# ScalarE's share of two chunk steps one tile behind VectorE's, squares and Hadamard steps by single tiles, and a Newton iteration moved from GpSimd to ScalarE

## Chip, cores and metric

One core of one Trainium2 chip runs the whole kernel. The metric is the device time of one execution in microseconds, lower is better. TensorE is called PE, VectorE DVE, ScalarE ACT and GpSimd POOL, as in the profile; SP is the engine that issues most DMAs.

## What is computed

The input x is (4, 512, 512) in float32. It is layer-normed to xn, and the output is `x + xn + mamba2(xn) + ffn(xn)`:

```python
z, xBC, dt = split(xn @ w_in)                  # 1024, 1280, 16 columns
xBC = silu(causal_conv4(xBC) + conv_b)         # x heads 1024, B 128, C 128
dt = softplus(dt + dt_bias)
y = ssd(xh * dt, dt * A, B, C) + xh * D        # a scan, in chunks
y = y * silu(z)
y = y * rsqrt(mean(y * y) + 1e-5) * norm_w
mamba = y @ w_out
ffn = (fwht(silu(xn @ W1.T) * (xn @ W3.T))) @ W2.T     # 2048 hidden columns
```

The Walsh-Hadamard transform (`fwht`) is folded into W2 once.

## The kernel before

**Precision.** Products run on PE in three float16 matmuls per float32 product (`three`, line 600): high by high, high by low, low by high. Each weight tile is scaled by a power of two, which comes from sums of squares of a group of tiles: steps `SQ` square raw tiles on ACT (line 1008), `QS` reduces them on PE and makes the scale on DVE (`to_scale`, signal `scale_13`). Then ACT writes the high half of a tile (`split_hi`, line 924) and DVE the low half (`split_lo`, line 1194), four tiles ahead of PE. This is done in batch 0 only; batches 1 to 3 load the split tiles back (66 of them).

**Tiles.** Per batch there are 10 `C` tiles (convolved columns; numbers 8 and 9 are B and C), 8 `Z` tiles (the gate), 16 pairs `A`, `U` (FFN gate and up) and 16 steps `G` (FFN down). A tile of the first four kinds is 12 matmuls of 128x512, about 2.6 us of PE. A `C` tile is evicted by ACT (line 968), by three taps on DVE (line 1244), then tanh on ACT (line 983) and a product on DVE (line 1229); a `Z` or `A` tile by tanh on ACT (line 973) and a product on DVE (lines 1255, 1260); a `U` tile by a product on DVE (line 1265), its high half on ACT (line 978) and the low half on POOL (line 1443). From the middle of a batch on three PSUM banks rotate for them.

**Steps.** Between the tiles stand steps, each with one part per engine:
- `DT`, `DTL`, `SUM`: dt, in the order PE, DVE (line 1146), ACT (lines 865, 867), POOL; then `DTL` with Ln on ACT, behind a load of its function table (line 871), and DVE's lines 1153 to 1161, whose last gives `dt_a`; `SUM` is PE's cumulative sums of it (lines 634 to 638, waiting on `dt_a`) and ACT's exponentials, for which `F0` waits (`ecst_ok`).
- `F0` to `F7` and `H0` to `H15`: the Hadamard transform of W2 in two passes. `H` is one matmul on bank 4 (line 751), evicted by ACT (line 1028) and DVE (line 1324). `H` number i waits on PE until `H` number i-1 is evicted.
- For each chunk c of 128 rows: `T` transposes, `X` exponentials, `S` and `R` states, `E`, `ES` decay rows, `Y` output (DVE gates it, lines 1365 and 1368; ACT squares it, line 1083), `N`, `Q`, `V` norms (ACT scales y, line 1087), `ROW` three Newton steps of 1/sqrt on one column (POOL), `W` the product with w_out (24 matmuls on the shared bank 3).
- `WOQ`, `WOS`, `WOH`: squares, scale and halves of w_out (line 1333 is the low half, 8 of them). `LN`, `XT` prepare the next batch: `LN` is DVE's statistics (lines 1120 to 1131) and ACT's normalisation (line 853, four operations).

**The order** is one list for all engines, `SCHEDULES[b]`. For batch 0 its head is written out in `FIRST`; after that a step stands at a tile number, out of `FIRST_AT`, `STEP_FIRST`, `ES_FIRST` and `PREP_FIRST`, and steps of one tile number are sorted by a rank (`LN` and `H` have the same rank and then sort by name, so an `H` of tile number 35 stands ahead of `LN`, one of 36 behind it). Every engine walks the list in this order, each instruction in its queue, and waits on semaphores where it needs another's work. Batches 1 to 3 use `STEP_AT` in the same way.

Of the kernel before, what the change touches and what calls it, by code (L numbers as in the profile page):

```python
# [216 lines left out]
def build(nc, x, w_in, w_dt, w1, w3, w2, w_out, conv_w, conv_b, dt_bias, a_log, d_cols, norm_w, consts, out):  # L217
# [6 lines left out]
    with ctx:  # L224
# [664 lines left out]
        def _(act):  # L889
# [49 lines left out]
            for b in range(NB):  # L939
# [45 lines left out]
                for kind, i in SCHEDULES[b]:  # L985
# [11 lines left out]
                    elif kind == "SQ":  # L997
                        act.wait_ge(d_quad[i], 32)
                        if i == 0:
                            act.wait_ge(sq_g1, G1_ACT)  # L1000
# [2 lines left out]
                        junk = sq_act[i >= QUADS_EARLY]
                        for half_of in range(2):
                            if i not in (0, QUADS_EARLY):
                                act.wait_ge(sq_quads, 2 * i + half_of - 1)
                            column = SQ_Q + 2 * i + half_of
                            nc.scalar.activation(junk[:, half_of * 2 * TILE:(half_of + 1) * 2 * TILE].rearrange("p (s c) -> p s c", s=2),
                                                 raw_load_view(i, half_of), ACT.Square,
                                                 accum_out=row_sq[:, column:column + 1]).then_inc(sq_quads, 1)  # L1010
# [540 lines left out]
```

## Time and profile before

| | |
|---|---|
| median of 3 runs | 967.67 us (966.13 to 968.0) |
| the profiled execution's own time | 965.39 us |
| its span, first to last instruction | 963.6 us |
| PE, DVE, ACT, POOL busy | 934.7, 555.8, 391.4, 276.1 us |
| mean granted clock of TensorE | 0.996 of full |

Busy time is the sum of what an engine's instructions cover. An idle stretch in front of an instruction is put down to the one that released it. The durations of matmuls overlap, so starts are the better measure on PE.

### The profile page before, as it was taken

What the parts mean: (1) busy time and instruction counts of PE and PEld (TensorE: products, weight loads), DVE (VectorE), ACT (ScalarE), POOL (GpSimd) and SP (SyncE); (2) the same over time, 40 slices, a digit from 0 to 9 for tenths busy, and PEclk for the clock granted to TensorE, in tenths of its full rate; (3) what the DMA queues carried; (4) which work ended last, traced back from release to release, by engine and by line L of the source; (5) the groups of instructions that cost most, each with busy time, mean ns of one, the idle gap of its engine ahead of it and who ended that gap; (6) DMA issues with size and microseconds to landing.
All of it is one profiled execution on the core that took longest, in us unless ns stands there. A gap on an engine that the chain in (4) does not pass through costs nothing.

```text
span 963.6 us, 13435 instructions
## 1 busy us (share of the span) xinstructions
PE 934.7 (97%) x5000; PEld 469.3 (49%) x5000; DVE 555.8 (58%) x955; ACT 391.4 (41%) x690; POOL 276.1 (29%) x354
## 2 busy tenths in 40 slices
PE   9899987989899999999999999999999999999998
PEld 4444443545344445555454445555445445555543
DVE  7876588875534756556532766566451666575421
ACT  6678874533323445233221434233222444343200
POOL 0000446352000116466110106565210104654410
PEclk9999999999999999999999999999999999999999
DMA  9798355434224335525223435436223435256123
GB/s 336 247 349 295 112 192 193 131 124 137 96 74 147 125 111 159 155 72 176 88 67 113 143 99 164 145 97 175 78 76 101 143 107 160 65 151 153 45 77 98
DMA packets 76208, 134.26 MB, mean 139 GB/s; under 512 B 7536, under 2 KB 20464, under 8 KB 74096
## 3 DMA queue, kind: packets, MB, share of 16 engines
q1 hardware_dynamic: 56640, 104.88, 34.1%
q10 hardware_dynamic: 19504, 28.53, 10.0%
q8 instruction: 40, 0.66, 0.3%
q14 instruction: 24, 0.20, 0.1%
HBM read 107.43 MB, written 25.95 MB: 138 GB/s over the span
## 4 chain that ended last, share of the span: by engine, by line
PE 67%; DVE 1%; DMA 1%; ACT 1%; issue 0%; DVEq 0%; ACTq 0%
PE ps L600 46%; PE ps L834 14%; PE ps L796 2%; PE ps L782 1%; PE ps L788 1%; PE ps L768 1%; DMA arena<-cs_rows 1%; PE ps L619 0%; PE ps L638 0%; PE ps L751 0%; PE ps L771 0%; DVE arena L1348 0%; DVE arena L1426 0%; ACT arena L1059 0%; DVE arena L1265 0%
## 5 line engine op out<-in xcount | busy, mean ns | idle before, releaser
L600 PE MATMUL ps<-xh,arena 128*128 128x512 f16 x1592 | 487.9, 379 | 3.4 <-DVE arena L1194 3.3
L600 PE MATMUL ps<-xl,arena 128*128 128x512 f16 x796 | 302.0, 379 | 0.0
L600 PEld LDWEIGHTS ps<-xh,arena 128*128 128x128 f16 x1592 | 158.3, 99 | 190.3 <-issue 5.9
L834 PE MATMUL ps<-arena 128*128 128x512 f16 x768 | 171.1, 379 | 0.0
L1443 POOL TENSOR_TENSOR arena<-arena 128x512 f16<-128x512 f32 x64 | 71.2, 1113 | 334.6 <-ACT arena L978 334.6
L1244 DVE SCALAR_TENSOR_TENSOR arena<-ps,cw,arena 128x511 f32<-128x511 f32 (+2 forms) x120 | 89.4, 747 | 66.9 <-ACT arena L968 65.0
L600 PEld LDWEIGHTS ps<-xl,arena 128*128 128x128 f16 x796 | 77.9, 98 | 88.7 <-issue 3.3
L834 PEld LDWEIGHTS ps<-arena 128*128 128x128 f16 x768 | 74.1, 98 | 91.2 <-issue 5.5
L978 ACT ACTIVATE arena<-arena 128x512 f16<-128x512 f32 x64 | 40.2, 629 | 141.3 <-DVE arena L1265 141.3
L1260 DVE SCALAR_TENSOR_TENSOR arena<-arena,ps 128x512 f32<-128x512 f32 x64 | 44.0, 687 | 77.3 <-ACT arena L973 77.0
L600 PE MATMUL ps<-wo_hi,arena 128*128 128x512 f16 x256 | 79.9, 384 | 3.6 <-DVE wo_lo L1333 3.4
L973 ACT ACTIVATE arena<-ps,f 128x512 f32<-128x512 f32 x64 | 43.4, 678 | 85.0 <-PE ps L600 85.0
L1454 POOL TENSOR_TENSOR arena<-arena 128x1024 f32<-128x1024 f32 x16 | 30.7, 1920 | 112.5 <-DMA arena<-cs_rows 112.5
L1265 DVE SCALAR_TENSOR_TENSOR arena<-ps,arena 128x512 f32<-128x512 f32 x64 | 44.1, 689 | 24.6 <-PE ps L600 23.3
L1348 DVE TENSOR_TENSOR arena<-arena 128x2048 f32<-128x2048 f32 x16 | 40.5, 2528 | 19.9 <-ACT arena L1074 19.9
L600 PE MATMUL ps<-wo_lo,arena 128*128 128x512 f16 x128 | 49.3, 385 | 0.0
L600 PEld LDWEIGHTS ps<-wo_hi,arena 128*128 128x128 f16 x256 | 25.3, 99 | 37.1 <-DVE wo_lo L1333 3.9
L1059 ACT ACTIVATE arena<-arena 128x128 f32<-128x128 f32 x128 | 40.5, 389 | 5.8 <-DMA arena<-cs_rows 5.8
L1194 DVE SCALAR_TENSOR_TENSOR arena<-arena,scl 128x512 f16<-128x512 f32 x50 | 38.7, 778 | 5.8 <-ACT arena L924 5.8
L924 ACT ACTIVATE arena<-arena,scl 128x512 f16<-128x512 f32 x50 | 35.3, 711 | 12.8 <-DVE f L1308 5.9
L968 ACT ACTIVATE arena<-ps,cb,cw 128x512 f32<-128x512 f32 x40 | 30.8, 771 | 23.1 <-PE ps L600 22.1
L1426 DVE SCALAR_TENSOR_TENSOR arena<-ps,f_w,arena 128x512 f32<-128x512 f32 x16 | 10.9, 745 | 50.3 <-PE ps L834 50.3
(179 smaller groups left out, 1092.8 us busy)
## 6 DMA issues: line engine op xcount, KB each, us to landing
arena<-w_parts SPq DMA_DIRECT2D x198, 256.0 KB, 2.6
w_parts<-arena SPq DMA_DIRECT2D x66, 256.0 KB, 2.6
arena<-cs_rows ACTq DMA_DIRECT2D x16, 1024.0 KB, 5.7
arena<-w SPq DMA_DIRECT2D x24, 512.0 KB, 4.9
arena<-ecs_rows ACTq DMA_DIRECT2D x24, 256.0 KB, 6.9
arena<-x ACTq DMA_DIRECT2D x18, 256.0 KB, 3.4
w_mid<-arena SPq DMA_DIRECT2D x8, 512.0 KB, 3.5
arena<-w_mid SPq DMA_DIRECT2D x16, 256.0 KB, 2.6
```

The lines of the kernel that those rows point to most:

```text
L600: ins = nc.tensor.matmul(out_ap, lhs(i, a), rhs(i, c), start=(i == 0 and s == 0), stop=(i == n - 1 and s == 2))
L834: ins = nc.tensor.matmul(bank(t), hw[a][:, i, t * P:(t + 1) * P], w2s[i % W2R][:, d, :], start=(i == 0 and s == 0), stop=(i == JF - 1 and ...
L924: nc.scalar.activation(part_hi[p % PARTS], raw_tile(p), ACT.Copy, scale=scl[:, n:n + 1]).then_inc(w_hi.sem, 1)
L973: nc.scalar.activation(slot, src, ACT.Tanh, scale=f_half[:, 0:1] if kind == "Z" else f_13[:, i // 2:i // 2 + 1]).then_inc(tanh_ok.sem, 1)
L978: nc.scalar.activation(hid_hi[:, i, :], hs[i % 2], ACT.Copy).then_inc(hid_h.sem, 1)
L1059: ins = nc.scalar.activation(Eb[:, h, :], csbc[:, h, :], ACT.Relu, scale=-1.0, bias=cs_s[:, c * NH + h:c * NH + h + 1])
L1194: nc.vector.scalar_tensor_tensor(out=part_lo[p % PARTS], in0=raw_tile(p), scalar=scl[:, n:n + 1], in1=part_hi[p % PARTS], op0=ALU.mult, op ...
L1244: ins = nc.vector.scalar_tensor_tensor(out=a[:, s:L], in0=src[:, 0:L - s], scalar=cw[:, i, TAPS - 1 - s:TAPS - s], in1=a[:, s:L], op0=ALU. ...
L1260: nc.vector.scalar_tensor_tensor(out=hs[i % 2], in0=tb[tanh[key] % 2], scalar=1.0, in1=src, op0=ALU.add, op1=ALU.mult).then_inc(evac.sem, 1)
L1265: nc.vector.scalar_tensor_tensor(out=hs[i % 2], in0=src, scalar=HID / (2 * XS * XS), in1=hs[i % 2], op0=ALU.mult, op1=ALU.mult).then_inc(e ...
L1348: nc.vector.tensor_tensor(Eb, Eb, Gm.unsqueeze(1).to_broadcast([P, NH, P]), ALU.mult).then_inc(m_ok.sem, 1)
L1443: nc.gpsimd.tensor_tensor(hid_lo[:, i, :], hs[i % 2], hid_hi[:, i, :], ALU.subtract).then_inc(hid_l.sem, 1)
```

## The change

In the head of batch 0, `DT` goes from in front of `C2` to behind it, `DTL` from behind `C2` to behind `Z1`, and `SUM` from behind `C4` to in front of it. A step `SQ` is now one half (two tiles) of what it was, so there are 16, and the second half stands one or two tiles behind the first. The Hadamard steps `H` stand at tile numbers 31 to 46, one each (before 30 to 46, two at 35 and none at 36 and 37). ACT's parts of `Y` and `N` are steps of their own, `YS` and `NS`, which in batch 0 stand behind `Y` and `N` by a tile; in batches 1 to 3 they stand at the same place. `QS6` moves ahead of `R1` (tile 18), `W0` goes from 18 to 19, `N1` and `Q1` from 20 to 21, and PE's waits follow: `W0` waits for `scale_13` at 7 and not 6. `ROW` moves from POOL (12 operations) to ACT (9), in all batches.

```diff
-FIRST = ("B G1S C C0 G1N C1 Z0 DT C2 DTL Z1 C3 Z2 C4 SUM Z3 WOL F0 C5 F1 SQ0 Z4 F2 C6 F3 QS0 Z5 F4 C7 F5 SQ1 Z6 F6 Z7 F7 QS1 E0 A0").split()
+FIRST = ("B G1S C C0 G1N C1 Z0 C2 DT Z1 DTL C3 Z2 SUM C4 Z3 WOL F0 C5 F1 SQ0 Z4 SQ1 F2 C6 F3 QS0 Z5 F4 C7 F5 SQ2 Z6 SQ3 F6 Z7 F7 QS1 E0 A0").split()
...
-            [("SQ", 2, 1), ("QS", 2, 3), ("SQ", 3, 4), ("QS", 3, 7), ("SQ", 4, 8), ("QS", 4, 12), ("SQ", 5, 11), ("QS", 5, 14),
-             ("SQ", 6, 16), ("QS", 6, 20), ("SQ", 7, 20), ("QS", 7, 23)] +
+            [("SQ", n, at) for n, at in enumerate((1, 2, 4, 5, 7, 8, 11, 12, 15, 16, 19, 20), 4)] +
+            [("QS", q, at) for q, at in enumerate((3, 7, 12, 14, 18, 23), 2)] +
...
-            [("H", j, at) for j, at in enumerate((30, 31, 32, 33, 34, 35, 35, 38, 39, 40, 41, 42, 43, 44, 45, 46))])
+            [("H", j, at) for j, at in enumerate(range(31, 31 + JF))])
...
-              "Y": (9, 17, 26, 34), "N": (12, 20, 28, 37), "Q": (12, 20, 28, 37), "V": (14, 23, 30, 39), "W": (18, 25, 31, 41),
-              "ROW": (15, 24, 31, 40)}
+              "Y": (9, 17, 26, 34), "YS": (10, 18, 27, 35), "N": (12, 21, 28, 37),
+              "NS": (13, 22, 29, 38), "Q": (12, 21, 28, 37), "V": (14, 23, 30, 39), "W": (19, 25, 31, 41), "ROW": (15, 24, 31, 40)}
...
                         elif i == 6:
-                            pe.wait_ge(mamba_evac.sem, mamba_evac.at(0, 0))
+                            pe.wait_ge(mean_read.sem, mean_read.at(0, 0))
...
-                            pe.wait_ge(scale_13, 6)
+                            pe.wait_ge(scale_13, 7)
...
+                    elif kind == "ROW":
+                        act.wait_ge(guess_ok.sem, guess_ok.at(b, c))
+                        for n in range(3):
+                            k = steps.step(nc.scalar.activation(ntmp, nr, ACT.Square))
+                            act.wait_ge(steps.sem, k)
+                            k = steps.step(nc.scalar.activation(ntmp, ntmp, ACT.Identity, scale=nmh, bias=three_halves[:, 0:1]))
+                            act.wait_ge(steps.sem, k)
+                            ins = nc.scalar.activation(nr, ntmp, ACT.Copy, scale=nr)
+                            if n < 2:
+                                k = steps.step(ins)
+                                act.wait_ge(steps.sem, k)
+                        ins.then_inc(root_ok.sem, 1)
...
-                    elif kind == "Y":
+                    elif kind == "YS":
...
-                    elif kind == "N":
+                    elif kind == "NS":
```

The order on DVE at the head of batch 0, from the silu product of `C0` on, before the change (line 1244 is the taps of `C2`, line 1146 `DT`, lines 1153 to 1161 `DTL`, line 1255 the eviction of `Z1`, line 1194 the splits):

```order
L1229 SCALAR_TENSOR_TENSOR arena<-arena 128x512
L1146 SCALAR_TENSOR_TENSOR arena<-ps,f_in,dtb 128x64
L1244 SCALAR_TENSOR_TENSOR arena<-ps,cw,arena 128x511
L1229 SCALAR_TENSOR_TENSOR arena<-arena 128x512
L1244 SCALAR_TENSOR_TENSOR arena<-ps,cw,arena 128x510
L1244 SCALAR_TENSOR_TENSOR arena<-ps,cw,arena 128x509
L1194 SCALAR_TENSOR_TENSOR arena<-arena,scl 128x512
L1153 RECIPROCAL arena<-arena 128x64
L1155 TENSOR_TENSOR arena<-arena 128x64
```

And in the changed kernel, whose line numbers are 12 or 13 higher here (1242 for 1229, 1257 for 1244, 1158 for 1146, 1268 for 1255, 1165 for 1153):

```order
L1242 SCALAR_TENSOR_TENSOR arena<-arena 128x512
L1257 SCALAR_TENSOR_TENSOR arena<-ps,cw,arena 128x511
L1242 SCALAR_TENSOR_TENSOR arena<-arena 128x512
L1257 SCALAR_TENSOR_TENSOR arena<-ps,cw,arena 128x510
L1257 SCALAR_TENSOR_TENSOR arena<-ps,cw,arena 128x509
L1207 SCALAR_TENSOR_TENSOR arena<-arena,scl 128x512
L1158 SCALAR_TENSOR_TENSOR arena<-ps,f_in,dtb 128x64
L1268 SCALAR_TENSOR_TENSOR arena<-arena,ps 128x512
L1207 SCALAR_TENSOR_TENSOR arena<-arena,scl 128x512
L1165 RECIPROCAL arena<-arena 128x64
L1167 TENSOR_TENSOR arena<-arena 128x64
```

`DT` stands behind all of `C2` and its split, and `DTL` behind `Z1` and another split.

The order on ACT at the end of batch 0, before: exponentials `X3` (lines 1072, 1074), `H3` and `H4`, the square of `Y3` (1083), `H5` and `H6`, the normalisation of `LN1` (853), `N3`'s scaling of y (1087), and the other `H`:

```order
L1072 ACTIVATE arena<-arena 128x1024
L1074 ACTIVATE arena<-arena 128x1024
L1028 ACTIVATE arena<-ps,f_had 128x512 x2
L1083 ACTIVATE arena<-arena 128x1024
L1028 ACTIVATE arena<-ps,f_had 128x512 x2
L853 ACTIVATE arena<-arena 128x512 x4
L1087 ACTIVATE arena<-arena 128x1024
L1028 ACTIVATE arena<-ps,f_had 128x512 x5
```

And in the changed kernel (1084 and 1086 for 1072 and 1074, 1095 for 1083, 855 for 853, 1099 for 1087):

```order
L1084 ACTIVATE arena<-arena 128x1024
L1086 ACTIVATE arena<-arena 128x1024
L1028 ACTIVATE arena<-ps,f_had 128x512 x3
L855 ACTIVATE arena<-arena 128x512 x4
L1095 ACTIVATE arena<-arena 128x1024
L1028 ACTIVATE arena<-ps,f_had 128x512 x3
L1099 ACTIVATE arena<-arena 128x1024
L1028 ACTIVATE arena<-ps,f_had 128x512 x2
```

The three ahead of the normalisation are now `H2` to `H4`; `H5` and the square of `Y3` stand behind it.

## Rows read from the trace of the kernel before

**Rows 1.** The page, busy us, share of the span, instructions of each engine

```profile
PE 934.7 (97%) x5000; PEld 469.3 (49%) x5000; DVE 555.8 (58%) x955; ACT 391.4 (41%) x690; POOL 276.1 (29%) x354
```

**Rows 2.** Stretches of 24 us: length, busy PE, PEld, DVE, ACT, POOL, clock, DMA, GB/s

```profile
24.00:48.00 24.00, 20.57 (x138) 9.75 (x138) 19.96 (x39) 16.47 (x26) 1.11 (x3) 1.00 0.72 247
...
120.00:144.00 24.00, 20.09 (x103) 11.79 (x104) 19.61 (x41) 16.93 (x35) 10.59 (x7) 0.93 0.60 191
144.00:168.00 24.00, 18.43 (x98) 8.48 (x97) 19.97 (x24) 12.53 (x21) 14.11 (x18) 0.93 0.59 193
...
312.00:336.00 24.00, 24.00 (x113) 10.92 (x112) 17.47 (x25) 12.16 (x23) 3.26 (x2) 1.00 0.42 138
```

**Rows 3.** Timeline of PE, front: start, duration, line, and the idle time before

```profile
42.33 0.38 PE L600 MATMUL ps<-xh,arena 128*128 128x512 f16 x1
45.08 0.39 PE L600 MATMUL ps<-xh,arena 128*128 128x512 f16 x1 [2.37 <-DVE arena L1194]
...
53.73 1.96 PE L719 MATMUL ps<-arena,hads 128*128 128x512 f32 x4 [1.60 <-issue]
```

**Rows 4.** Timeline of ACT, front, from the tanh step of C1 to Ln

```profile
39.20 0.63 ACT L983 ACTIVATE arena<-arena 128x512 f32<-128x512 f32 x1 [3.27 <-DVE arena L1229]
39.73 0.24 ACT L865 ACTIVATE arena<-arena 128x64 f32<-128x64 f32 x1
40.00 0.26 ACT L867 ACTIVATE arena<-arena 128x64 f32<-128x64 f32 x1
40.17 0.71 ACT L924 ACTIVATE arena<-arena,scl 128x512 f16<-128x512 f32 x1
40.78 0.76 ACT L968 ACTIVATE arena<-ps,cb,cw 128x512 f32<-128x512 f32 x1
41.56 1.28 ACT L871 ACT_TABLE_LOAD   x1
42.85 0.26 ACT L871 ACTIVATE arena<-arena 128x64 f32<-128x64 f32 x1
```

**Rows 5.** Timeline of DVE, front: the taps of C2, then DTL

```profile
41.57 0.75 DVE L1244 SCALAR_TENSOR_TENSOR arena<-ps,cw,arena 128x511 f32<-128x511 f32 x1 [2.22 <-ACT arena L968]
...
44.94 0.54 DVE L1153 RECIPROCAL arena<-arena 128x64 f32<-128x64 f32 x1
...
45.66 0.22 DVE L1157 SCALAR_TENSOR_TENSOR arena<-arena 128x64 f32<-128x64 f32 x1
...
46.17 0.23 DVE L1161 TENSOR_TENSOR arena<-arena,nega 128x64 f32<-128x64 f32 x1
```

**Rows 6.** Timeline of PE, middle: the first product with w_out, the tile after

```profile
160.53 0.50 PE L600 MATMUL ps<-wo_hi,arena 128*128 128x512 f16 x1 [3.43 <-DVE wo_lo L1333]
...
167.41 0.38 PE L600 MATMUL ps<-xh,arena 128*128 128x512 f16 x1
```

**Rows 7.** ACT's squares in the groups by line (busy, mean ns); DVE's timeline, middle

```profile
L1008 ACT ACTIVATE arena<-arena 128x1024 bf16<-128x1024 f32 x16 | 16.7, 1045 | 0.0
...
127.05 0.75 DVE L1194 SCALAR_TENSOR_TENSOR arena<-arena,scl 128x512 f16<-128x512 f32 x1 [1.29 <-ACT arena L924]
...
159.73 0.74 DVE L1333 SCALAR_TENSOR_TENSOR wo_lo<-arena,nws,wo_hi 128x512 f16<-128x512 f32 x1
...
162.84 0.68 DVE L1265 SCALAR_TENSOR_TENSOR arena<-ps,arena 128x512 f32<-128x512 f32 x1
```

**Rows 8.** Timeline of PE, tail: the H matmuls that wait

```profile
216.00 1.10 PE L751 MATMUL ps<-arena,hads 128*128 128x512 f32 x2 [2.31 <-issue]
...
245.27 1.13 PE L751 MATMUL ps<-arena,hads 128*128 128x512 f32 x2 [1.62 <-DVE arena L1324]
...
258.85 1.12 PE L751 MATMUL ps<-arena,hads 128*128 128x512 f32 x2 [1.07 <-DVE arena L1324]
```

**Rows 9.** Timelines of DVE and ACT, tail: LN1's first step, the normalisation

```profile
247.82 2.46 DVE L1120 BATCH_NORM_STATS2 arena<-arena 128x6 f32<-128x512 f32 x4
...
253.47 2.94 ACT L853 ACTIVATE arena<-arena 128x512 f32<-128x512 f32 x4 [6.35 <-DVE arena L1131]
```

More of the change, by code:

```diff
@@ L62 @@
     "Y": (6, 14, 22, 32),
+    "YS": (6, 14, 22, 32),
     "N": (8, 16, 24, 34),
+    "NS": (8, 16, 24, 34),
     "Q": (8, 16, 24, 34),
@@ L233, in build @@
         ident, tri_le, tri_gt, ones = (con[:, i * P:(i + 1) * P] for i in range(4))
-        cmean = sb("cmean", [P, 1])
+        cmean, three_halves = sb("cmean", [P, 1]), sb("three_halves", [P, 1])
         hads = sb("hads", [P, 2 * P])
@@ L997, in _ @@
                     elif kind == "SQ":
-                        act.wait_ge(d_quad[i], 32)
+                        quad, half_of = divmod(i, 2)
+                        act.wait_ge(d_quad[quad], 32)
                         if i == 0:
                             act.wait_ge(sq_g1, G1_ACT)
-                        elif i == QUADS_EARLY:
+                        elif i == 2 * QUADS_EARLY:
                             act.wait_ge(xt_done.sem, xt_done.at(0, MC - 1))
[L1003 to L1010, printed above, removed]
+                        if quad not in (0, QUADS_EARLY):
+                            act.wait_ge(sq_quads, i - 1)
+                        junk = sq_act[quad >= QUADS_EARLY][:, half_of * 2 * TILE:(half_of + 1) * 2 * TILE]
+                        nc.scalar.activation(junk.rearrange("p (s c) -> p s c", s=2), raw_load_view(quad, half_of), ACT.Square,
+                                             accum_out=row_sq[:, SQ_Q + i:SQ_Q + i + 1]).then_inc(sq_quads, 1)
                     elif kind == "F":
@@ L1166, in _ @@
             steps = Steps(dve_steps)
+            nc.vector.memset(three_halves[:], 1.5)
             nc.vector.memset(row_sq[:], 2.0 ** -60).then_inc(guards, 1)
@@ L1299, in _ @@
                         dve.wait_ge(quad_sums, i + 1)
-                        if i in (4, 6):
-                            dve.wait_ge(pe_tot.sem, pe_tot.at(0, i // 6))
+                        if i == 4:
+                            dve.wait_ge(pe_tot.sem, pe_tot.at(0, 0))
                         elif i in (5, 7):
@@ L1477, in _ @@
                         nc.gpsimd.tensor_tensor(de, dm, de, ALU.subtract).then_inc(dt_u.sem, 1)
-                    elif kind == "ROW":
-                        pool.wait_ge(guess_ok.sem, guess_ok.at(b, c))
-                        for n in range(3):
-                            k = newton.step(nc.gpsimd.tensor_tensor(ntmp, nr, nr, ALU.mult))
-                            pool.wait_ge(newton.sem, k)
-                            k = newton.step(nc.gpsimd.tensor_tensor(ntmp, ntmp, nmh, ALU.mult))
-                            pool.wait_ge(newton.sem, k)
-                            k = newton.step(nc.gpsimd.tensor_scalar(ntmp, ntmp, 1.5, None, ALU.add))
-                            pool.wait_ge(newton.sem, k)
-                            ins = nc.gpsimd.tensor_tensor(nr, ntmp, nr, ALU.mult)
-                            if n < 2:
-                                k = newton.step(ins)
-                                pool.wait_ge(newton.sem, k)
-                        ins.then_inc(root_ok.sem, 1)
                     elif kind == "S" and c > 0:
```

## The prediction

> **What bounds the kernel now.** I read the page first, then the busy times by stretch, then TensorE's own timeline. TensorE is busy for 934.7 of 963.6 us [rows 1], so at most 28.9 us can be won while its work stays the same. The stretches say where they lie [rows 2]: in 312:336 PE is busy for all of 24.00 us, and every such stretch from there to 936:960 shows 23.8 or more; only the first batch has holes, as 20.57 busy in 24:48, 20.09 in 120:144 and 18.43 in 144:168. So batches 1 to 3 can only lose, and I follow batch 0's waits one by one: the front (before 60), the middle (110 to 170), the tail (215 to 290).
>
> **Front: `SUM` a tile early, `DT` and `DTL` a tile late.** Before, PE waits 2.37 us ahead of tile `C4` (45.08), runs `SUM`, `Z3`, and starts `F0` at 53.73 [rows 3]. The chain that feeds `SUM` was off PE's path: DVE did `DT` right after its eviction of `Z0`, and ACT had the result when it came to it. Now DVE takes all of `C2` first, and PE asks for the result after `Z2`, whose last matmul ends at 42.33 + 0.38 = 42.71. Step by step:
> - ACT ends the tanh step of `C1` as before; `DT`'s two small operations (39.73 to 40.17, 0.44) no longer stand ahead of the split and the first tap of `C2`, which starts at 40.34 and ends at 41.1 [rows 4].
> - DVE's `C2` with its split takes 44.94 - 41.57 = 3.37 [rows 5], so `DT` starts on DVE at 44.5. It lasts about 0.3 (an estimate: no row here has it apart from ACT's 0.26 for the same 64 columns), and ACT, idle since 41.1, goes on at 44.8.
> - ACT: `DT` 0.44, the split 0.61, two tanh steps of about 0.55 each (`C1`'s occupies 39.73 - 39.20 = 0.53), the table load with Ln 1.29 + 0.26 [rows 4]: Ln ends at 44.8 + 3.7 = 48.5.
> - DVE's last three of `DTL` take 46.17 + 0.23 - 45.66 = 0.74 [rows 5]: `dt_a` at 49.3, and PE starts `SUM` at about 49.4 instead of 42.7: **a wait of 6.7 us where 2.37 stood**.
> - `SUM` (1.7, an estimate: from 45.08 to 53.73 lie `C4`, `SUM`, `Z3` and 1.60 of wait, so 8.65 - 1.60 - 2 x 2.65), `C4` and `Z3` end 7.0 later, at 56.4; their weights are long split by then. `F0` starts there instead of 53.73, without its old wait of 1.60. Front: **+2.7 us**. ACT and DVE are held by PE again at `F0` to `F7`, so all behind moves with it.
>
> The table load bears on this chain. In the row the load begins at 41.56, takes 1.28, and Ln starts 1.29 after it [rows 4]. The Trainium skill ("ScalarE: Activation LUTs", What ACT_TABLE_LOAD costs) adds a drain of about 1.38 us to each switch; the trace does not agree, since the operation ahead of the load ended only just before it. By the page the wait would be 1.4 longer, and the sum below +5.5.
>
> **Middle: squares by half, `YS0` behind `WOS0`, `W0` behind `A9`.** PE waits here for DVE and ACT: it misses 3.9 us of 120:144 and 5.6 of 144:168 [rows 2], 3.43 of them ahead of `W0` at 160.53 [rows 6]. Up to DVE's `WOH7` (159.73) the change frees three things: half a square (1.05 [rows 7], 1.04 in occupancy) ahead of `WOQ7`; DVE's wait of 1.29 at 127.05, where the split stood on ACT behind `Y0`'s square; and half a square ahead of `WOH6`: s = 3.4 us. In exchange `W0` now needs `scale_13` at 7, so DVE must first do `Y1`, `U8`, a split and `QS6`: `U8`'s eviction starts at 162.84, and it, the split and the five small operations of `QS6` take 0.6 + 0.7 + 0.7, which ends 4.4 us beyond the end of `WOH7` (159.73 + 0.74) [rows 7]. `W0` so starts at 160.5 + 4.4 - 3.4 = 161.5, about 1.0 later, but `A9` (2.6) and `QS6` (0.35) are already done on PE: **-1.9 us**. Bounds of s: 1.3 (the one wait that is named) gives +0.2; 8, were nearly all of the 9.5 us that PE misses there to go, gives -6.5. I take 3.4, the sum of what is seen to leave the path. The wait ahead of `W0` stays long (3.6), so its low clock stays in.
>
> **Tail: `H0` to `H5` a tile later, `H5` behind `LN1`.** `H0`'s wait of 2.31 (216.00) goes, since `A15` now covers it; so do 1.62 ahead of old `H6` and 1.07 ahead of `H8` [rows 8]. But DVE and ACT now do `LN1` between `H4` and `H5`, and PE issues `H6` only when `H5` is evicted. Place by place, on before's clock with the earlier start (PE is 3.4 ahead at `A15`, and pays `H0` of 0.86 later): `Y3` starts at 234.7, `G2` 236.6, `H4` 239.25, `G3`, `H5` 242.7, `G4` ends at 246.2. `H4` is evicted 2.3 after its start, at 241.6; `LN1` on DVE takes 5.6, from 247.82 until ACT begins behind it at 253.47 [rows 9], so to 247.2; from there ACT's normalisation, `YS3`'s square (it took the place of the 1.04 of `NS3`), the two evictions and PE need 258.85 - 253.47 = 5.4, as before's `H8` shows [rows 8, 9]: `H6` at 252.6, **a wait of 6.4 us**. Then `G5`, `H7`, `G6`, and `H8` at 259.7 instead of 258.85: **+0.9 us**.
>
> **Clock.** In 144:168 the granted clock is 0.93 [rows 2]: the half level, 1.2 GHz, for a stretch behind the wait of 3.43, 0.07 x 24 = 1.7 us lost (`W0` takes 167.41 - 160.53 = 6.9 [rows 6]). Behind the waits of 6.7 and 6.4 I expect the same; nothing hides it there, since PE is then the bound. Part of a low stretch can fall into the wait, so I take 1.2 each, **+2.4**, from bounds of 0 and 3.4. The Trainium skill ("TensorE: Matmul & The Clock Gate", Part 1) says the same way that an idle array is gated to 1.2 GHz until it is busy again; it speaks against a change that gathers short waits into a long one, and its half rate gives the same 1.7 at most.
>
> **Newton on ACT.** Nine dependent activations of one column instead of twelve operations on POOL. The nearest row is the pair at 39.73 and 40.00 [rows 4], a step of 0.27: 2.4 us of ACT sixteen times. In batches 1 to 3 ACT is idle for half of 312:336 [rows 2] and PE for nothing; cover is the slack of 3 banks. I take 0, from 0 to +2.
>
> **Sum.** 2.7 - 1.9 + 0.9 + 2.4 + 0 = **+4.1 us**. The profiled execution took 965.39 (span 963.6 and 1.8 around it), so it would take 969.5; the median of the three runs, 967.67, lies 2.3 above it, and I set the forecast against that: **971.8 us**.
>
> **Rivals.**
> - *Both long waits come, as above*: +4.1, chance 0.60, its own range +1.5 to +7.5 (969.2 to 975.2).
> - *The middle gives back more* (faster): its place is DVE's chain from `WOS0` to `QS6`. If s is 8, the sum is 4.1 - 4.6 = -0.5; to be measurably faster it must exceed 9.4, all of PE's waits there. For it: DVE and ACT are what PE waits for. Against: `QS5` and `V0` still need DVE's sum of squares. Chance 0.08 for a faster result and 0.08 for one that only cancels.
> - *One of the two long waits isn't there*: if `dt_a` comes by 42.7, the front is -4.0 instead of +3.9 and the result 963.9; if `H5` is not held by `LN1`, the tail is -5.5 instead of +2.1 and the result 964.2. For it: a single row read wrongly in the order. Against: both waits follow from one queue's order. Chance 0.08.
> - *The parts cancel*: without low clock and with a front of +1.5, +0.5, 968.2; chance 0.08.
> - *The lag stays in ACT and DVE as well* (they leave the front 3.4 late and not 2.7, and the squares of batch 0 are then late too), with the full low clock: +8, 975.7; chance 0.05. By the page's drain at each switch, 973.2; chance 0.03, since the row speaks against it.
>
> **Numbers.** The runs of this kernel tell a difference from none at about 0.2%, 1.9 us. Slower by more: 0.60 + 0.05 + 0.03, less the low end of the first, 0.67. Within: 0.17. Faster: 0.16. The range takes in the cancelling cases and the late lag, and leaves out the cases with a wait missing: 967.0 to 976.5.
>
> **What would show it.** A PE wait near 43 of 6 to 7 us that DVE's `DTL` ends, with `F0` at 56.4; `W0` behind `A9`, about 161.5 plus the front's shift; no wait ahead of `H0`; a wait of 6.4 ahead of the seventh H matmul; a granted clock below 1 in 48:72 and near 255; batches 1 to 3 as long as before. I am wrong if the first or the fourth is missing, or if the stretch 120 to 180 loses more than 6 us.

## The result, and the profile after

The changed kernel takes 977.26 us (median of 6 runs, 972.95 to 978.4), the kernel before 967.66 in the same comparison (6 runs): a ratio of 1.0092, with a 95% interval of 1.0074 to 1.011. It is slower by 9.6 us, where 4.1 were forecast and 976.5 was the end of the range. The profiled execution took 977.51, its span is 975.7, 12.1 more than before. One of the six executions of run e12 below took 4006.22 us and is left out of its ratio; the other five took 975.1 to 976.0.

The page of the changed kernel, busy us of each engine (before: [rows 1]):

```profile
PE 939.8 (96%) x4999; PEld 472.1 (48%) x5000; DVE 558.4 (57%) x956; ACT 433.6 (44%) x834; POOL 227.9 (23%) x162
```

PE does the same matmuls and is busy 5.1 us longer, and idle 975.7 - 939.8 = 35.9 us instead of 28.9. So of the 12.1, 5.1 is the same work at a lower clock, and 7.0 is waiting.

The stretches of the changed kernel, with the granted clock as third number from the end (before: [rows 2]):

```profile
24.00:48.00 24.00, 17.65 (x122) 8.14 (x122) 18.51 (x34) 12.71 (x22) 1.06 (x3) 0.99 0.75 249
48.00:72.00 24.00, 22.38 (x87) 11.01 (x88) 16.62 (x29) 20.17 (x35) 0.00 (x0) 0.86 0.77 272
120.00:144.00 24.00, 20.06 (x118) 11.35 (x116) 17.77 (x41) 17.81 (x35) 10.32 (x7) 0.93 0.67 209
144.00:168.00 24.00, 19.29 (x118) 10.69 (x118) 23.80 (x34) 15.83 (x32) 7.27 (x4) 1.00 0.45 133
168.00:192.00 24.00, 22.52 (x111) 11.69 (x111) 14.53 (x27) 13.82 (x28) 10.23 (x7) 0.93 0.53 184
240.00:264.00 24.00, 17.60 (x89) 8.43 (x88) 11.26 (x37) 6.60 (x10) 2.35 (x1) 0.83 0.25 85
264.00:288.00 24.00, 24.00 (x104) 11.35 (x102) 8.20 (x15) 7.39 (x17) 0.00 (x0) 0.95 0.31 102
```

In two stretches, 24:48 and 240:264, PE now misses 6.35 and 6.40 us (3.43 and 2.69 before), and the clock falls behind each wait. In 144:168 DVE is busy for 23.80 of 24 (19.97 before): there it is now the engine that PE waits for.

PE's timeline of the changed kernel, the places that the prediction spoke of (before: [rows 3, 6, 8]); lines are 2 higher than before, so 636 is `SUM`, 721 `F`, 602 a tile or `W`, 809 `N`, 753 `H`:

```profile
49.62 0.69 PE L636 MATMUL ps<-arena,con 128*128 128x64 f32 x2 [6.76 <-DVE arena L1173]
...
58.90 1.45 PE L721 MATMUL ps<-arena,hads 128*128 128x512 f32 x3
...
169.48 0.38 PE L602 MATMUL ps<-wo_hi,arena 128*128 128x512 f16 x1 [4.22 <-issue]
...
214.16 0.38 PE L809 MATMUL ps<-arena,con 128*128 128x1 f32 x2 [1.61 <-ACT arena L1095]
...
259.95 2.07 PE L753 MATMUL ps<-arena,hads 128*128 128x512 f32 x2 [6.40 <-DVE arena L1337]
...
270.15 1.02 PE L753 MATMUL ps<-arena,hads 128*128 128x512 f32 x2
...
311.05 0.33 PE L636 MATMUL ps<-arena,con 128*128 128x64 f32 x2
...
655.44 0.38 PE L602 MATMUL ps<-wo_hi,arena 128*128 128x512 f16 x1 [1.14 <-DVE arena L1403]
```

`N2` and `SUM` of batch 1 in the kernel before (807 is `N`, 634 is `SUM`):

```profile
206.89 0.38 PE L807 MATMUL ps<-arena,con 128*128 128x1 f32 x2 [0.41 <-ACT arena L1083]
...
299.90 0.33 PE L634 MATMUL ps<-arena,con 128*128 128x64 f32 x2
```

Read down, this is the account of the 12.1 us. `F0` is 5.2 later than before (58.90 - 53.73). `N2` (214.16) stood at 206.89, so it is 7.3 late: the middle added 2.1. `SUM` of batch 1 (311.05) stood at 299.90, 11.15 late: the tail added 3.9. The rest of the program adds 0.95, nearly all of it in the last row, a new wait in batch 2.

### The profile page after: what moved, and what is told of

Read it like the earlier page. It is cut to its first block, busy times and chain, and to the rows that moved or that the text cites. A ratio compares the mean times of both kernels' runs of the same rounds, so it can differ in the third digit from the quotient of the medians.

```text
span 975.7 us, 13392 instructions
## 1 busy us (share of the span) xinstructions
PE 939.8 (96%) x4999; PEld 472.1 (48%) x5000; DVE 558.4 (57%) x956; ACT 433.6 (44%) x834; POOL 227.9 (23%) x162
## 4 chain that ended last, share of the span: by engine, by line
PE 66%; DVE 1%; DMA 1%; ACT 1%; issue 0%; DVEq 0%; ACTq 0%
PE ps L602 45%; PE ps L836 14%; PE ps L798 2%; PE ps L784 1%; PE ps L790 1%; PE ps L770 1%; DMA arena<-cs_rows 1%; PE ps L621 0%; PE ps L640 0%; PE ps L753 0%; PE ps L773 0%; DVE arena L1361 0%; DVE arena L1439 0%; ACT arena L1059 0%; DVE arena L1278 0%
## 5 line engine op out<-in xcount | busy, mean ns | idle before, releaser
L836 PE MATMUL ps<-arena 128*128 128x512 f16 x768 | 173.2, 382 | 0.0
L1207 DVE SCALAR_TENSOR_TENSOR arena<-arena,scl 128x512 f16<-128x512 f32 x50 | 42.1, 846 | 2.5 <-ACT arena L926 2.5
```

The source lines that it names most:

```text
L836: ins = nc.tensor.matmul(bank(t), hw[a][:, i, t * P:(t + 1) * P], w2s[i % W2R][:, d, :], start=(i == 0 and s == 0), stop=(i == JF - 1 and ...
L1207: nc.vector.scalar_tensor_tensor(out=part_lo[p % PARTS], in0=raw_tile(p), scalar=scl[:, n:n + 1], in1=part_hi[p % PARTS], op0=ALU.mult, op ...
```

## The experiments

The kernel before was measured again beside each group of runs (medians 967.2 for e1 to e4, 967.66 for e5 to e8, 966.61 for e9 to e11, 966.44 for e12 to e15, 966.6 for e16), so the ratios are the measure. "Batch 1" is the start of its `SUM` in the profiled execution, which shows what batch 0 cost in that one execution. It lies up to 3 us below the run's median (e4 977.07 of 980.02, e11 958.29 of 960.62), so a difference of 2 or 3 in this column proves nothing by itself.

| run | what it is | median us | ratio to before (95%) | batch 1 |
|---|---|---|---|---|
| before | | 967.66 | 1 | 299.90 |
| changed | | 977.26 | 1.0092 (1.0074 to 1.011) | 311.05 |
| e1 | changed, front undone | 971.29 | 1.0043 (1.003 to 1.0055) | 305.11 |
| e2 | changed, `H` undone | 978.23 | 1.0104 (1.0087 to 1.0121) | 312.16 |
| e3 | changed, both undone | 973.4 | 1.0061 (1.0049 to 1.0074) | 306.39 |
| e4 | changed, Newton on POOL | 980.02 | 1.0129 (1.011 to 1.0148) | 311.14 |
| e5 | e3, `YS3`, `NS3` undone | 965.11 | 0.9979 (0.9964 to 0.9994) | 299.75 |
| e6 | e5, `W0`, `QS6` undone | 961.09 | 0.994 (0.9919 to 0.996) | 295.19 |
| e7 | before, only `H` | 968.66 | 1.0018 (1.0005 to 1.0031) | 302.33 |
| e8 | before, only Newton | 964.54 | 0.9976 (0.9962 to 0.9989) | 297.61 |
| e9 | e6, `YS`, `NS` undone | 966.26 | 0.9989 (0.9977 to 1.0001) | 299.72 |
| e10 | e6, `DT`, `DTL` late | 963.07 | 0.9965 (0.9953 to 0.9977) | 297.96 |
| e11 | e6, `W0` behind `A9` | 960.62 | 0.9942 (0.9928 to 0.9955) | 292.87 |
| e12 | changed, `YS3`, `NS3` undone | 975.56 | 1.0096 (1.0076 to 1.0115) | 308.98 |
| e13 | changed, `W0`, `QS6` undone | 971.77 | 1.0054 (1.0038 to 1.0071) | 305.08 |
| e14 | before, only the front | 972.75 | 1.0066 (1.0048 to 1.0085) | 305.79 |
| e15 | e11, `QS5`, `V0` later | 964.16 | 0.9972 (0.996 to 0.9984) | 297.86 |
| e16 | e6, narrow POOL products | 959.58 | 0.9918 (0.9895 to 0.9941) | 295.07 |

### The front and the H steps undone (e1, e2, e3), the Newton steps back (e4)

```diff
-FIRST = ("... Z0 C2 DT Z1 DTL C3 Z2 SUM C4 Z3 ...")
+FIRST = ("... Z0 DT C2 DTL Z1 C3 Z2 C4 SUM Z3 ...")            # e1, e3
-            [("H", j, at) for j, at in enumerate(range(31, 31 + JF))])
+            [("H", j, at) for j, at in enumerate((30, 31, 32, 33, 34, 35, 35, 38, 39, 40, 41, 42, 43, 44, 45, 46))])   # e2, e3
```

e4 puts the twelve operations of `ROW` back into POOL's part, as in the diff of the change.

> The changed kernel with DT, DTL and SUM back where they stood before the change; half squares, YS, NS, the middle, the H steps and the Newton steps on ScalarE stay. Theory A (the two long waits, each with a stretch of half clock behind it, make nearly all of the loss; the front's share is what F0 shows, 58.9 instead of 53.7): the wait of 6.8 at SUM goes, F0 starts at 53.7 to 54.2, no low clock in 48:72, and the time falls by 5 us against the changed kernel, to about 972. Rival B (the loss comes from the work that ScalarE now does at other places, half squares, YS and NS and Newton steps, and the front is only where it shows): F0 stays later than 56 and the time falls by under 2 us. Rival C (the middle takes up a shift of the front, so the front's loss is hidden behind it): F0 falls by 5, but the gain is gone by 180, and the time stays within 1.5 us of the changed kernel.

> The changed kernel with the H steps back at the tile numbers that they had before (30 to 35, two at 35, then 38 to 46), so that H5 stands ahead of LN1 again; all else as changed. Theory A: the wait of 6.4 ahead of the seventh H matmul goes, and with it the half clock behind it; the old waits of 2.3, 1.6 and 1.1 come back; batch 1 starts 5 to 7 us earlier than in the changed kernel and the time falls by 5 to 7, to about 971. Rival B (the LN1 of the next batch is late in any case because YS3 and NS3 now stand elsewhere): a wait of over 4 us stays in 245:265, and the time falls by under 2.

> The changed kernel with both undone: DT, DTL, SUM and the H steps as before the change; half squares, YS and NS a tile behind, W0 behind A9 and the Newton steps on ScalarE stay. Theory A, additive: the time falls by 10 to 12 against the changed kernel, to 965 to 968, level with the kernel before within 0.2% (the middle worth between -2 and +1). Rival B (the other parts carry a good share): it stays over 970. Rival C (the two low clock stretches are one affair, the first makes the second): then undoing the front alone would give as much as undoing both.

> The changed kernel with the three Newton steps back on GpSimd in all four batches; all else as changed. Theory A: no difference beyond 1.2 us (ScalarE has idle time to spare, the chain of nine takes 2.9 there and twelve take 3.3 on GpSimd); at most the wait of 1.14 at 655 in batch 2 goes. Rival B (nine dependent steps block ScalarE's queue sixteen times, and the evictions behind them are late for TensorE): the time falls by 3 us or more, spread over the batches.

Theory A of e1 held: 1.0092 falls to 1.0043, `F0` starts at 53.81, and batch 1 starts 5.9 earlier. For the tail rival B held, in e2 and in e3: with `H` as before the time is no better (1.0104), and a wait of 5.89 is still there; e3 ends at 973.4 and not at 965 to 968. PE's and ACT's timelines of e3 (855 is `LN1`'s normalisation, 1095 the square of `Y3`):

```profile
256.24 0.59 PE L809 MATMUL ps<-arena,con 128*128 128x1 f32 x2 [5.89 <-ACT arena L1095]
```

```profile
252.22 2.93 ACT L855 ACTIVATE arena<-arena 128x512 f32<-128x512 f32 x4 [6.35 <-DVE arena L1143]
255.05 1.04 ACT L1095 ACTIVATE arena<-arena 128x1024 f32<-128x1024 f32 x1
```

`YS3` stands behind `LN1` on ACT too, and `N3` needs it. The wait of 6.4 had two causes, each of which is enough for most of it; taking one away moved it one step on. e4 went against both of its theories: back on POOL, the kernel is not faster but slower (1.0129), though the two intervals touch at 1.011. In its trace `W0` waits 4.72 and `N2` 2.75 (4.22 and 1.61 in the changed kernel).

### The lag of YS3 (e5), the middle (e6)

```diff
-"YS": (10, 18, 27, 35)   "NS": (13, 22, 29, 38)
+"YS": (10, 18, 27, 34)   "NS": (13, 22, 29, 37)      # e5
-"W": (19, 25, 31, 41)    "N", "Q": (12, 21, 28, 37)   ("QS", 6, 18)   pe.wait_ge(scale_13, 7)
+"W": (18, 25, 31, 41)    "N", "Q": (12, 20, 28, 37)   ("QS", 6, 20)   pe.wait_ge(scale_13, 6)   # e6
```

e6 also puts `NS1` at 21 and restores PE's and DVE's waits of before around `QS6`.

> The kernel of the run with both undone, and YS3 and NS3 back at tile numbers 34 and 37, so that ScalarE squares y ahead of the normalisation of LN1. With both undone the tail still had a wait of 5.89, now ahead of N3, ended by that square. Theory A (two changes each make the tail wait by themselves, H5 behind LN1 and YS3 behind LN1, so that undoing one moved the wait and won nothing): the wait of 5.9 and the low clock of 0.86 in 240:264 go, SUM of batch 1 starts at 299 to 300.5 instead of 306.4, and the time is 966 to 968, level with the kernel before. Rival B (the tail is late because LN1 itself comes late): a wait of over 4 stays in 240:265 at another matmul, and the time falls by under 2 from 973.4.

> The same, and in the middle W0 back at 18, QS6 and N1 and Q1 at 20, with PE's waits of before; what stays of the change is the half squares, YS0 to YS2 and NS0 to NS2 a tile behind, and the Newton steps on ScalarE. Theory A (the middle is held by VectorE's queue, whose work is the same, so that nothing is won or lost there by W0's place): within 1 us of the run above. Rival B (W0 behind A9 hides 1.9 as predicted, and the lag elsewhere eats it): slower than the run above by 1.5 to 3. Rival C (needing QS6 ahead of W0 costs): faster by 1.5 to 3.

Theory A of e5 held: the ratio fell from 1.0061 to 0.9979. The stretch 240:264 in e3 and then in e5:

```profile
240.00:264.00 24.00, 16.54 (x58) 6.85 (x57) 10.54 (x35) 6.24 (x10) 0.00 (x0) 0.86 0.14 45
```

```profile
240.00:264.00 24.00, 21.30 (x90) 9.42 (x91) 14.47 (x41) 8.13 (x12) 0.00 (x0) 1.00 0.30 102
```

PE has 4.8 us back and the clock is full. e6 fell again, to 0.994, by 0.39% or 3.8 us, which is rival C's direction and more than its 1.5 to 3. The first product of `W0` starts at 159.22 in e6. The edit is a bundle, `W0` behind `QS6`'s scale and `N1`, `Q1` a tile later; e11 below shows that `W0`'s place behind `A9` costs nothing without `QS6`'s scale, but `N1` and `Q1` were not tried alone.

### One part alone on the kernel before (e7, e8, e14)

e7 has only the list of `H` steps of the change, e8 only `ROW` on ACT, e14 only the new `FIRST` order of `DT`, `DTL` and `SUM`.

> The kernel before with only the H steps at 31 to 46, everything else as before. Theory A: the tail wait needs no help from the other edits: a wait of 6 to 6.5 ahead of the seventh H matmul, low clock behind it, H8 at 262 to 263, the old waits of 2.31 and 1.62 gone, and the time 3 to 5 us over the kernel before, 970 to 972. Rival B (the wait needs YS3 behind LN1 as well): under 968.5.

> The kernel before with only the three Newton steps on ScalarE, in all batches. Theory A: no difference beyond 1 us. Rival B (nine dependent steps hold back ScalarE's evictions in the middle of batch 0, where TensorE waits for ScalarE and VectorE): slower by 1.5 to 3. Rival C (the chain is shorter, 2.9 instead of 3.3, and GpSimd's queue is freed): faster by 1.5 to 3, as the run with the steps back on GpSimd hinted, which was 2.7 over the changed kernel.

> The kernel before with only DT, DTL and SUM at their changed places. Theory A: a wait of 6.8 at SUM, F0 at 58.5 to 59, a granted clock of 0.85 to 0.9 in 48:72, the time 5 to 6 over the kernel before, 972 to 973.5. Rival B (the kernel of before has slack in its middle that takes up a late front): under 970. Rival C (the clock's stretch falls elsewhere): F0 at 56.5 and 970 to 971.

e7 shows the tail's wait without any help, 5.41 long where 6 to 6.5 were expected, but it costs only +0.18% (1.7 us), less than theory A's 3 to 5: the waits of 2.31 and 1.62 that it fills are gone. e14 repeats the front, with the same wait of 6.76 and `F0` at 58.63, and costs 6.4 us, a little over theory A. PE's timelines of the two:

```profile
252.06 1.22 PE L751 MATMUL ps<-arena,hads 128*128 128x512 f32 x1 [5.41 <-DVE arena L1324]
```

```profile
49.71 0.69 PE L634 MATMUL ps<-arena,con 128*128 128x64 f32 x2 [6.76 <-DVE arena L1161]
...
58.63 0.59 PE L719 MATMUL ps<-arena,hads 128*128 128x512 f32 x1
```

e8 was a gain of 0.24%, where I had none; rival C of its expectation held. From 129 to 148 DVE and ACT of e8 run as in e7, 0.11 to 0.12 us earlier throughout, and what differs next is `ROW0`. POOL and DVE of e7, with Newton on POOL (1348 and 1333 are DVE's decay product and a low half of w_out, 1495 and 1497 POOL's two products of the state step, which stand behind `ROW0` in its queue):

```profile
150.13 2.12 POOL L1481 TENSOR_TENSOR arena<-arena 128x1 f32<-128x1 f32 x1
...
154.60 2.35 POOL L1495 TENSOR_TENSOR arena<-arena 128x1024 f32<-128x1024 f32 x1
156.91 1.90 POOL L1497 TENSOR_TENSOR arena<-arena 128x1024 f32<-128x1024 f32 x1
```

```profile
149.91 2.28 DVE L1348 TENSOR_TENSOR arena<-arena 128x2048 f32<-128x2048 f32 x1
...
157.32 2.04 DVE L1333 SCALAR_TENSOR_TENSOR wo_lo<-arena,nws,wo_hi 128x512 f16<-128x512 f32 x1 [2.73 <-ACT wo_hi L1037]
```

A one-column square takes 2.12 us on POOL, until DVE's product (149.91 to 152.19) is over; `ROW0` so takes 6.5 us in all (148.13 to 154.64), and POOL's products, late by it, run into the low half, which takes 2.04 instead of 0.74. In e8 they start at 153.30 and meet the split ahead of it instead (2.48), which costs little, since DVE waited for ACT behind that split anyway; the low half takes 1.32, and `W0` starts at 160.74 instead of 161.57. With the shift taken off, 0.7 us is won there and 1.3 by `N2`; the rest of e8's 2.3 us was not traced.

### Half squares and lag apart (e9); POOL's products (e16)

e9 is e6 with `YS` at (9, 17, 26, 34) and `NS` at (12, 20, 28, 37), beside `Y` and `N`. e16 leaves part of chunk 1's state and y in batch 0 out of the computation:

```diff
-nc.gpsimd.tensor_tensor(XD, XD, t1, ALU.add)
+nc.gpsimd.tensor_tensor(XD[:, 0:w], XD[:, 0:w], t1[:, 0:w], ALU.add)     # w = 16 for b == 0 and c == 1, the decay alike
```

> The kernel of the run with the middle undone as well (961.1), and YS0 to YS2 and NS0 to NS2 back beside Y and N. What stays of the change is the half squares and the Newton steps on ScalarE. Theory A (the half squares ahead of WOQ7 and WOH6 are what the middle gained, W0 at 159.2 instead of 160.5 to 161.6): within 1 us of 961. Rival B (the lag is what freed VectorE's wait of 1.29 at 127 and gained): 2 to 3 us slower, near 964, which is where the kernel with Newton alone on ScalarE stood.

> The kernel with the middle undone (961.1), in which GpSimd's two products of chunk 1 in batch 0 (XD plus t1, and the decay of the state, 128x1024 each) work on 16 columns instead of 1024; so part of the state and of y is left out of the computation in that chunk, and the time tells only what these two do to others. In the trace of that kernel they last from 151.78 to 156.46 and VectorE's split that starts at 152.22 takes 2.47 and the low half of w_out after it 2.35, where the same instructions take 0.74 elsewhere. Theory A (the two engines exclude each other: a VectorE instruction with two inputs from SBUF does not proceed while GpSimd's runs): both take 0.74, VectorE gets 3.3 us of its queue back, is held next by ScalarE's high halves, and W0 starts 0.6 to 2 us earlier; the time falls by 0.5 to 2. Rival B (they are slow for another reason, a late semaphore or a stretch of slow clock on all engines): they stay above 2 us, and the time stays within 0.5.

Rival B of e9 held, and by more: the lag of `YS0` to `YS2` and `NS0` to `NS2` is worth 0.49% (4.7 us). With it the waits ahead of `QS4` (3.55, now 1.56), `Y1` (2.25, now none) and `H0` (2.23, now none) shrink; those ahead of `QS5` and `V0` grow by 2.0 together. The half squares without the lag show no gain (e9 is 0.13% over e8, with intervals that overlap): PE's wait ahead of `WOS0` goes, and a longer one ahead of `W0` takes its place.

e16 shows what else stood in DVE's way. DVE and POOL in e6:

```profile
152.22 2.47 DVE L1207 SCALAR_TENSOR_TENSOR arena<-arena,scl 128x512 f16<-128x512 f32 x1
154.65 2.35 DVE L1346 SCALAR_TENSOR_TENSOR wo_lo<-arena,nws,wo_hi 128x512 f16<-128x512 f32 x1
...
158.42 0.74 DVE L1346 SCALAR_TENSOR_TENSOR wo_lo<-arena,nws,wo_hi 128x512 f16<-128x512 f32 x1
```

```profile
151.78 2.36 POOL L1494 TENSOR_TENSOR arena<-arena 128x1024 f32<-128x1024 f32 x1 [8.33 <-DVE arena L1366]
154.10 2.36 POOL L1496 TENSOR_TENSOR arena<-arena 128x1024 f32<-128x1024 f32 x1
```

and DVE in e16:

```profile
152.25 0.74 DVE L1207 SCALAR_TENSOR_TENSOR arena<-arena,scl 128x512 f16<-128x512 f32 x1
154.68 0.75 DVE L1346 SCALAR_TENSOR_TENSOR wo_lo<-arena,nws,wo_hi 128x512 f16<-128x512 f32 x1 [1.69 <-ACT wo_hi L1037]
```

Both instructions fall to 0.74 and 0.75: theory A's mechanism is shown. Its price is not: `W0` starts at 158.99, 0.23 earlier than in e6, because DVE then waits for ACT, 1.69 for a high half and 1.48 for a tanh step; the intervals of e6 and e16 overlap.

### The front by half (e10); W0 and the last waits of the middle (e11, e15)

```diff
+FIRST = ("... Z0 C2 DT Z1 DTL C3 Z2 C4 SUM Z3 ...")          # e10
+"W": (19, 25, 31, 41), with QS6 at 20 and scale_13 at 6       # e11
+("QS", 5, 15)   "V": (15, ...)   "ROW": (16, ...)             # e15, on e11
```

> The same kernel (961.1) with DT behind C2 and DTL behind Z1 as in the changed kernel, but SUM left behind C4 where it was. Theory A (the front's loss needs both: dt_a comes at 49.3 by VectorE's queue, and SUM a tile early turns it into a wait of 6.8 with nothing in front of it; behind C4 the same lateness meets a wait of 1.5 to 4 after a tile that is done): SUM starts at 49.4 with C4 done by then, F0 at 53.5 to 54.5, time within 1.5 us of 961. Rival B (the lateness of dt_a alone costs what was lost): F0 at 56 or later and the time at 964 to 967.

> The same kernel (961.1) with W0 alone moved from 18 to 19, behind the tile A9 as in the changed kernel, but with QS6 left behind it at 20, so that W0 needs only the sixth scale. Theory A (in the changed kernel it was the scale of QS6 on VectorE that held W0, not its place): W0 starts behind A9 at 159 to 160, its wait of 2.71 is filled by A9, QS6 comes at the same place, and the time falls by 1.5 to 3, to 958 to 959.5. Rival B (what follows W0 on VectorE, its eviction and QS6, gets later by the same tile, so the wait only moves on): within 1 us of 961. Rival C: slower by 2 or more, as when W0 stood behind both.

> The kernel with W0 alone behind A9 (960.6), and QS5 and V0 at 15 instead of 14 and ROW0 at 16, since TensorE waited 2.60 ahead of QS5 for VectorE's scale of y and 0.86 ahead of V0. Theory A: both waits are filled by the tile A7, and the time falls by 1 to 3.5, to 957.5 to 959.5. Rival B (VectorE is the bound from 120 to 165, and the fifth scale comes later for the splits behind it): the waits only move on, within 1 us of 960.6 or slower.

e10 came between its two theories, at +0.25% over e6 (2.4 us). Theory A's place was right, as PE's timeline shows: `SUM` at 49.56 with `C4` done. But `F0` is at 57.20, as rival B had it:

```profile
49.56 0.62 PE L636 MATMUL ps<-arena,con 128*128 128x64 f32 x2 [2.06 <-DVE arena L1173]
...
57.20 1.02 PE L721 MATMUL ps<-arena,hads 128*128 128x512 f32 x2
```

In 48:72 the granted clock is 0.86, behind two waits of 1.94 (ahead of `C4`) and 2.06 in place of one of 6.76. From the start of `SUM` to the end of `Z3` lie 7.6 us (49.56 to 57.20), and 4.3 in the kernel before (47.67 to about 52.0), so the low clock costs 3.3 here:

```profile
48.00:72.00 24.00, 22.44 (x81) 10.78 (x81) 16.98 (x30) 21.17 (x36) 0.00 (x0) 0.86 0.83 296
```

e11 filled `W0`'s wait of 2.71 and has the earliest batch 1 of all, but 960.62 against 961.09 is no difference by its runs, so rival B held; `QS6` now waits 1.36. The 2.60 ahead of `QS5` do not come from the edit: `QS5` starts at 136.65 in e11 and at 136.63 in e6, where it waits 0.93, and PE only reached the place earlier. e15 filled the waits of `QS5` and `V0` and lost 0.30% (2.9 us), as its rival B allowed: it waits 3.33 ahead of `W0` and 4.32 ahead of `Y1`, where e11 has no wait:

```profile
152.03 3.58 PE L798 MATMUL ps<-arena 128*64 128x128 f32 x32 [4.32 <-DVE arena L1366]
```

### The tail and the middle on the changed kernel (e12, e13)

e12 makes e5's edit and e13 makes e6's edit on the changed kernel, alone.

> The changed kernel with YS3 and NS3 alone back at 34 and 37, everything else as changed. Theory A (two causes, each enough for the tail's wait: H5 behind LN1, and YS3 behind LN1): the wait ahead of the seventh H matmul stays, 5.4 instead of 6.4 because the square no longer stands between, and the time falls by 1 to 2.5, to 975 to 976. Rival B (YS3 is the cause, as its cost of 8.3 with the H steps of before suggests): the wait goes below 2 and the time falls by 6 or more, to 971.

> The changed kernel with W0, QS6, N1 and Q1 alone back where they stood. Theory A (needing the scale of QS6 costs 4 wherever the front stands): W0's wait falls from 4.2 to 2 to 3, and the time by 3 to 4.5, to 973 to 974. Rival B (in the changed kernel the lost time of the middle overlaps with the tail's wait, which then starts earlier and grows): the time falls by under 1.5.

In e12 theory A held for the wait, which stays, 5.42 long, and not for the time: the ratio does not move (1.0096 and 1.0092), where 1 to 2.5 us were expected. In e13 theory A held: the ratio falls by 0.38%, as from e5 to e6; `W0` waits 2.71, and `N2`'s wait of 1.61 is gone as well. PE's timelines of the two:

```profile
259.03 1.22 PE L753 MATMUL ps<-arena,hads 128*128 128x512 f32 x1 [5.42 <-DVE arena L1337]
```

```profile
165.02 0.39 PE L602 MATMUL ps<-wo_hi,arena 128*128 128x512 f16 x1 [2.71 <-DVE wo_lo L1346]
```

## Why the prediction was wrong, point by point

The direction and both long waits were right; the sum was wrong by 8 us of span. The largest part, 4.0, is the middle, where the step that failed is the value of s. The clock is 1.1 of the front's 1.3 and 1.9 in the tail, and 0.95 came in batches 1 to 3. The durations below are those of one profiled execution each.

- **Front, +3.9 forecast with its clock, +5.2 measured.** The wait is 6.76 (6.7 forecast) and starts `SUM` at 49.62 (49.4): the walk through DVE's and ACT's queues held. So did its reading of the table load: a drain of 1.38 more, which the Trainium skill ("ScalarE: Activation LUTs", What ACT_TABLE_LOAD costs) adds, would have put `SUM` near 51. What was mis-sized is the clock. From `SUM` to `F0` lie 9.28 us instead of 7.0, so the low clock cost 2.3 and not 1.2. In the other five traces with this front (e2, e4, e12, e13, e14) the same stretch takes 8.7 to 9.7, so the cost is 1.7 to 2.7. e14 measures the part alone at +0.66%, e1 its removal at -0.49%.
- **Middle, -1.9 forecast, +2.1 measured.** This step failed, in the value of s, the time by which DVE's `WOH7` comes earlier. DVE's last low half of w_out started at 159.73 before and should have come 3.4 earlier. In the changed kernel it comes at 164.22, which is 159.05 once the front's 5.17 are taken off: s is 0.7, below my lower bound of 1.3. The 4.4 us of DVE work between it and the scale of `QS6` were right (164.96 to 169.37, and `W0` at 169.48). DVE's timeline of the changed kernel (1207 and 1346 are low halves, 1321 the end of `QS6`'s scale):

```profile
158.01 2.48 DVE L1207 SCALAR_TENSOR_TENSOR arena<-arena,scl 128x512 f16<-128x512 f32 x1
160.44 2.36 DVE L1346 SCALAR_TENSOR_TENSOR wo_lo<-arena,nws,wo_hi 128x512 f16<-128x512 f32 x1
...
164.22 0.74 DVE L1346 SCALAR_TENSOR_TENSOR wo_lo<-arena,nws,wo_hi 128x512 f16<-128x512 f32 x1
...
169.22 0.15 DVE L1321 TENSOR_SCALAR f<-inv 128x1 f32<-128x1 f32 x1
```

I had added up what leaves the path and not asked what holds DVE next. The waits for ACT of 1.29 and 2.73 did go, and two low halves then met POOL's products (2.48 and 2.36 instead of 0.74 each); with that gone too (e16), ACT holds it. The remaining 1.2 is `N2`'s longer wait (1.61 for 0.41), of which the prediction had nothing and which is gone in e13. Undoing `W0` behind `QS6`, with `N1` and `Q1`, gives 0.38% on the changed kernel and 0.39% on e5. Without that bundle the middle is a gain (e6).
- **Tail, +2.1 forecast with its clock, +3.9 measured.** The wait is 6.40, as forecast. From `H6` to `H8` lie 10.2 us instead of 7.1, so the low clock cost 3.1 and not 1.2; this execution is the dearest, since in e1, e4, e7, e12 and e13 the same steps take 9.05 to 9.6. What the prediction also missed, without harm to its sum, is that `YS3` behind `LN1` makes the same wait by itself (5.89 ahead of `N3` in e3): it counted the square only as 1.04 in the chain behind `H5`. Both together cost 0.64% (e5 to e1), and `H` alone on the kernel before 0.18%. The likely reason is that only there the wait of 2.31 ahead of `H0` was still to be won, since with the lag it is gone already (2.23 in e9, none in e6); `H` alone on a kernel with the lag and without `YS3` was not run.
- **Clock, +2.4 forecast, about +5.4 measured.** This is 2.3 and 3.1 from above, and PE's busy time shows it independently, 939.8 against 934.7. I had carried 1.7 over from the stretch behind the wait of 3.43 and taken a part of it off. The bound of 3.4 for both together was too low as well. The Trainium skill ("TensorE: Matmul & The Clock Gate", Part 1) was right about the sign, that an idle array comes back at 1.2 GHz. The "1.7 at most" that the prediction worked out from its half rate was exceeded by both stretches.
- **Newton on ACT, 0 forecast from 0 to +2, a gain measured** (e8 -0.24%; e4 the other way, +0.37%, less sure). The chain of nine takes 2.9 us (0.98 for each of the three Newton steps), where the estimate was 2.4. The mistake was to cost only what ACT takes on, and nothing for what POOL gives up: twelve instructions that in `ROW0` stretch to 6.5 us under DVE's work and push POOL's products into the low half of w_out.
- **Batches 1 to 3, 0 forecast, +0.95 measured.** W1's product of batch 2 waits 1.14 (655.44). ACT stood 3.90 us before 641.92 for a transfer of decay rows, 1.0 longer than at the same place of the kernel before (2.92), and what it does for DVE is late by that. Waits on the same DVE line in batches 1 to 3 sum to 0.6 to 1.8 in e1 to e4, e12 and e14, to 0.5 and 0.7 in e15 and e16, and to 0.2 or nothing in the others. They go with no single edit and not with the end of batch 0 alone (e1 and e13 start batch 1 at the same time, 0.9 and none). What makes that transfer late stays open; it was not tried.

By spans the sum was off by 8.0, by medians by 5.5; the 2.5 between are the profiled executions, that of before 2.3 under its median and that of the changed kernel 0.25 over.

**The rivals.** "The middle gives back more" is refuted for this kernel. "One of the two long waits isn't there" and "The parts cancel" are out as well: both waits and both low stretches came. "The lag stays in ACT and DVE, with the full low clock" had 975.7 and the nearest number, but not by its mechanism: what the front lost beyond 2.7 is the clock on PE, not ACT and DVE staying back. Its +8 was not worked out either: 4.1, the front 0.7 later and a full low clock, 1.0 more, make 5.8, and no row gave the rest. Of what was to show the forecast right, the waits, the covered `H0` and the clock below 1 in 48:72 and near 255 all came; `W0` did not: 166.7 with the front's shift was forecast, and it started at 169.48. None of the three signs that the prediction named for being wrong appeared, the last included: PE is idle for 10.1 us of 120:180, and was for 9.5 before. So they could not have shown the error in the middle, which the place of `W0` shows.

**A version that beats both.** e6 takes the Newton steps on ACT, the half squares and the lag of `YS0` to `YS2` and `NS0` to `NS2`, and leaves the front, `H`, `YS3` and `W0` as they were: 0.994 (0.9919 to 0.996). e11 is level with it, 0.9942 (0.9928 to 0.9955).

## What to carry to other kernels

When several steps are moved past the same long block (here `LN1`), list every one of them: each may be enough for nearly the whole wait, and undoing one then shows nothing. A wait that an edit takes away is worth only the distance to the next engine in line, so sum what holds the waiting engine next, not what leaves. Cost the engine that is relieved as well as the one that is loaded, above all when GpSimd and VectorE both work on SBUF.
